# A fused attention-convolution and mixture-of-experts layer on one core: attention in blocks of five rows, all taps spread ahead of the first image, the normalised copy made where it is used

## What is computed

```python
# layer 0, first half: a convolution yields 49 weights per pixel, and these weigh a 7x7 window, dilation 2
u = ln_over_channels(x)
k = relu(conv7x7_dilated2(u, w1) + b1)              # 256 -> 128 channels
k = relu(batchnorm(conv1x1(k, w2) + b2))            # 128 -> 49
attn = softmax(k, axis=1)
out = sum(shift(u, 2*ki, 2*kj) * attn[:, p] for p, (ki, kj) in enumerate(taps))
x = x + out
# second half: tokens are pixels; each of the four batches picks two of eight experts from its mean token
t = tokens(x); tn = ln(t)
rw = softmax(scaled(softmax(mean(tn) @ Wr + br)))   # top 2 of 8, per batch
y = sum_k w_k * (gelu(tn @ W1[k] + b1[k]) @ W2[k] + b2[k])
x = t + ln(y + tn) * gamma + beta
```

## Time and profile before

| | |
|---|---|
| median of three runs | 1289.99 us (1288.7 to 1295.73) |
| profiled execution | 1290.51 us, span 1288.6 us |
| TensorE busy | 1128.8 us (88%) |
| VectorE busy | 715.9 us (56%) |
| ScalarE busy | 496.7 us (39%) |
| GpSimd busy | 237.4 us (18%) |
| mean granted clock of TensorE | 0.898 of 2.4 GHz |
| DMA | 106.34 MB, 83 GB/s on average |

### The profile page before, as it was taken

How to read it: one execution, slowest core, us unless ns; L and a number is a source line. 1 busy time by engine, 2 the same in 40 slices (tenths; PEclk the granted TensorE clock), 3 DMA queues, 4 the chain that set the end, 5 groups by cost and what they waited for, 6 DMA issues and landing times. The chain is left out here.

```text
span 1288.6 us, 19335 instructions
## 1 busy us (share of the span) xinstructions
PE 1128.8 (88%) x7380; PEld 980.9 (76%) x7380; DVE 715.9 (56%) x1719; ACT 496.7 (39%) x923; POOL 237.4 (18%) x160
## 2 busy tenths in 40 slices
PE   3766899999999999939877978689899989989997
PEld 2665667667666666639877968589899989989997
DVE  3445345356355243414673664456777776776776
ACT  4444333232332201114353354364454455455442
POOL 1000000000000000010251353203322331332332
PEclk9969899999999999755885687689999999999999
DMA  9210021112102000060894297404214211421211
GB/s 272 82 37 19 19 74 38 38 39 87 37 1 73 17 1 16 1 134 3 220 264 113 58 269 204 150 25 148 74 50 133 77 51 60 147 73 37 75 50 37
DMA packets 98968, 106.34 MB, mean 83 GB/s; under 512 B 5298, under 2 KB 95699, under 8 KB 98692
## 3 DMA queue, kind: packets, MB, share of 16 engines
q1 hardware_dynamic: 79888, 86.15, 23.4%
q10 hardware_dynamic: 19000, 19.11, 4.8%
HBM read 65.69 MB, written 39.56 MB: 82 GB/s over the span
## 5 line engine op out<-in xcount | busy, mean ns | idle before, releaser
L729 PE MATMUL pM<-V,U 128*128 128x368 f16 (+3 forms) x2016 | 319.3, 315 | 0.0
L729 PEld LDWEIGHTS pM<-V,U 128*128 128x128 f16 x2016 | 196.7, 98 | 107.2 <-issue 0.8
L1507 DVE TENSOR_TENSOR gl<-gf,gh 128x384 fp32r<-128x384 f32 x192 | 161.9, 864 | 63.6 <-ACT gh L1401 63.6
L1401 ACT ACTIVATE gf<-pH,b1c 128x384 f32<-128x384 f32 x192 | 112.0, 583 | 193.3 <-PE pH L1620 143.2
L1635 PE MATMUL pY<-w2h,gh 128*128 128x256 f32 x576 | 167.4, 291 | 17.4 <-DVE z L1519 16.4
L1635 PE MATMUL pY<-w2l,gh 128*128 128x256 f32 x576 | 163.1, 283 | 0.0
L1635 PE MATMUL pY<-w2h,gl 128*128 128x256 f32 x576 | 162.9, 283 | 0.0
L521 DVE TENSOR_TENSOR V<-pV,V 128x384 f16<-128x384 f32 x96 | 53.1, 556 | 179.7 <-ACT V L407 179.4
L1620 PE MATMUL pH<-xh,w1h 128*128 128x384 f32 x384 | 131.5, 343 | 9.3 <-DVE xl L1500 4.6
L407 ACT CAST V<-pV 128x384 f16<-128x384 f32 x96 | 45.6, 477 | 225.8 <-PE pV L700 225.7
L1620 PE MATMUL pH<-xl,w1h 128*128 128x384 f32 x384 | 130.7, 340 | 0.0
(11 more groups left out here) (173 smaller groups left out, 1539.2 us busy)
## 6 DMA issues: line engine op xcount, KB each, us to landing
xa<-in_xt SPq DMA_DIRECT2D x16, 576.0 KB, 5.0
xn_scratch<-xa SPq DMA_DIRECT2D x16, 576.0 KB, 6.0
xn<-xn_scratch SPq DMA_DIRECT2D x16, 576.0 KB, 8.6
xr<-in_xt SPq DMA_DIRECT2D x16, 576.0 KB, 6.3
t_scratch<-ts ACTq DMA_DIRECT2D x16, 576.0 KB, 5.3
tn_scratch<-tn ACTq DMA_DIRECT2D x16, 576.0 KB, 5.3
tnk<-tn_scratch SPq DMA_DIRECT2D x24, 384.0 KB, 3.3
tk<-t_scratch SPq DMA_DIRECT2D x24, 384.0 KB, 3.9
```

The costliest lines, as they stand in the source:

```text
L729: return nc.tensor.matmul(out[:, :, first:end], U[:, hi_u, k, piece, :], V[:, b % 2, hi_v, k, c, :, first + TILES * d:end + TILES * d], st ...
L1401: last = nc.scalar.activation(dst, pH[:, j % 4, 0:CN], ACT.Gelu, bias=b1c[:, j // FB, j % FB:j % FB + 1])
L1507: tt(gl[:, sl, j, :], gf[:, j % 2, :], gh[:, sl, j, :].bitcast(F32), ALU.subtract).then_inc(g_step, 1)
```

## The change

It has four parts.

- **Start-up of the convolution.** Tap turns and image turns alternate: tap turn j of a pair, then image turn j of the next image. The magnitudes, `ln`, `normalise_x` and `tap_scale` get fixed places between them. The batch-norm constants are made after pair 0. `bound` writes to another PSUM bank.
- **Attention blocks.** A block is five rows, 120 tokens (`TB`), and an image has five blocks, the last of four rows. There are 11 pairs (d, h) for 10, `SLOT` is 6 for 4, so a group of eight images has 44 items of six matmuls; `SBANKS` is 3. An image's `attend` has 39 matmuls for 48. Transfers of an image are split in two (four whole blocks and the short one).
- **Spreading first.** `A` has room for both groups. All 88 items are done before image 0; the load of the second group's taps waits for the last item of the first group. The lists in the image loop change: ScalarE `store(n-1)`, `normalise(n-1)`, `x_high(n+2)`; VectorE `sums(n)`, `x_low(n+2)`, `statistics(n)`. `accumulate` covers all images, with two buffers.
- **No `tn` in DRAM.** The attention phase no longer stores it. The expert phase makes `tnk` from `tk`: `statistics` on VectorE, `scale_x` on GpSimd, `normalise` on ScalarE, three chunks ahead. `tk` has three buffers.

The diff, cut to its core:

```diff
@@ conv_phase, VectorE (ScalarE and TensorE have the same form)
-            u_lows(0, 0, U_PAIR)
-            tap_scale(1)
-            v_lows(2)
-            ln(3)
...
+            tap_scale(0)
+            for pair in range(PAIRS_OG):
+                for j in range(U_PAIR):
+                    u_low(U_PAIR * pair + j)
+                    if j < V_TURNS and pair + 1 < BI:
+                        v_low(V_TURNS * (pair + 1) + j)
+                    if j == LN_AT and pair + 2 <= BI:
+                        ln(pair + 2)
+                    if j == SCALE_AT and pair + 1 < PAIRS_OG:
+                        tap_scale(pair + 1)
+                if pair == 0:
...
@@ constants of the attention
+BROWS = 5
+TB = BROWS * SIDE
+NB = -(-SIDE // BROWS)
-SLOT = 4
-SBANKS = OBANKS = 4
+SLOT = 6
+SBANKS, OBANKS = 3, 4
@@ attend_phase, SyncE
-            for n in range(IMGS):
-                if n % GI == 0 and n // GI + 1 < GROUPS:
-                    load_attn(n // GI + 1)
+            load_attn(1)
+            for n in range(2, IMGS):
+                load_xn(n)
+                load_x(n)
@@ attend_phase, ScalarE
-            for n in range(IMGS):
-                if n % GI == 0:
-                    spread_out(act, nc.scalar.copy, n // GI, 0, a_by_act, x_high)
-                    x_high(n + 1)
-                if (n + 1) % GI > 0 and n + 2 < IMGS:
-                    x_high(n + 2)
-                if n > 0:
-                    normalise(n - 1)
-                    store(n - 1)
+            for u in range(0, GROUPS * NU, 2):
+                spread_out(act, nc.scalar.copy, u, a_by_act)
+                if u == NU // 2:
+                    x_high(0)
+            x_high(1)
+            for n in range(IMGS):
+                if n > 0:
+                    store(n - 1)
+                    normalise(n - 1)
+                if n + 2 < IMGS:
+                    x_high(n + 2)
@@ attend_phase, VectorE
             for n in range(IMGS):
...
                 sums(n)
-                if (n + 1) % GI > 0:
-                    statistics(n)
-                    if n + 2 < IMGS:
-                        x_low(n + 2)
+                if n + 2 < IMGS:
+                    x_low(n + 2)
+                statistics(n)
@@ attend_phase, TensorE
+            for item in range(GROUPS * NU):
+                spread_taps(item)
             for n in range(IMGS):
-                if n % GI == 0:
-                    spread_taps(n // GI)
                 attend(n)
@@ ffn_phase, SyncE
-                sp.dma_start(tnk[:, s], tn_d[rows, :].rearrange("(t p) c -> p t c", p=P)).then_inc(tnk_loaded[s], 16)
                 sp.dma_start(tk[:, s], t_d[rows, :].rearrange("(t p) c -> p t c", p=P)).then_inc(tk_loaded[s], 16)
@@ ffn_phase, GpSimd
+                    if later(b, m, 3, CHUNKS):
+                        scale_x(*later(b, m, 3, CHUNKS))
                     rsqrt(b, m)
@@ ffn_phase, ScalarE
+            def normalise(b, m):
+                n, s = CHUNKS * b + m, m % 2
+                act.wait_ge(x_scaled, 2 * (n + 1))
...
+                for t in range(CT):
+                    last = nc.scalar.activation(tnk[:, s, t, :], tk[:, m % TBUFS, t, :], ACT.Identity,
+                                                bias=xsh[:, s, t:t + 1], scale=xrs[:, s, t:t + 1])
+                last.then_inc(tn_made, 2)
+            normalise(0, 0)
+            normalise(0, 1)
             take_x(0, 0)
             split_w1(0)
...
                     if later(b, m, 2, CHUNKS):
                         take_x(*later(b, m, 2, CHUNKS))
+                    if later(b, m, 3, CHUNKS):
+                        normalise(*later(b, m, 3, CHUNKS))
                     if m == CHUNKS - 2 and later(b, m, 2, CHUNKS):
                         split_w1(b + 1)
@@ ffn_phase, VectorE
+            def statistics(b, m):
...
+                for t in range(CT):
+                    s.did(nc.vector.bn_stats(xst[:, t, :], tk[:, m % TBUFS, t, :]))
+                s.settle()
+                carry(nc, spare[0:1, 0:1])
+                for t in range(CT):
+                    s.did(nc.vector.bn_aggr(xmv[:, t, :], xst[:, t, :]))
+                s.settle()
...
+                s.did(nc.vector.tensor_scalar(xve[:, sl], xmv[:, :, 1], 1e-5, None, ALU.add))
+                s.did(nc.vector.tensor_scalar(xnm[:, sl], xmv[:, :, 0], -1.0, None, ALU.mult))
...
                     if later(b, m, 2, CHUNKS):
                         take_x(*later(b, m, 2, CHUNKS))
+                    if later(b, m, 3, CHUNKS):
+                        statistics(*later(b, m, 3, CHUNKS))
                     if m == CHUNKS - 2 and later(b, m, 2, CHUNKS):
                         split_w1(b + 1)
                     sum_up(b, m)
```

More of the change, by code:

```diff
@@ L619, in a_low @@
                        ALU.subtract).then_inc(alo_ready, 1)
-            def v_lows(n):
-                for j in range(V_TURNS):
-                    v_low(V_TURNS * n + j)
-            def u_lows(pair, first, end):
-                for j in range(first, end):
-                    u_low(U_PAIR * pair + j)
             ln(0)
             ln(1)
-            v_lows(0)
-            ln(2)
-            v_lows(1)
-            dve.wait_ge(par_loaded, 16 * 7)
-            s = Steps(dve, bn_step, 0, BN_STEPS)
@@ L648, in _ @@
-            s.settle()
-            s.did(nc.vector.tensor_scalar(w2s[:, :], w2s[:, :], bnp[:, 7:8], None, ALU.mult))
-            s.did(stt(bnp[:, 0:1], bnp[:, 0:1], bnp[:, 7:8], bnp[:, 2:3], ALU.mult, ALU.add))
-            s.at(BN_STEPS)
-            u_lows(2, 0, U_HALF)
-            tap_scale(3)
-            u_lows(2, U_HALF, U_PAIR)
-            v_lows(3)
-            ln(BI)
-            u_lows(3, 0, U_PAIR)
+            for j in range(V_TURNS):
+                v_low(j)
+            tap_scale(0)
@@ new lines, in normalise @@
+                for t in range(NB):
+                    rows = rows_of(t)
+                    last = nc.scalar.activation(tn[0:rows, n % 2, t, :], ts_[0:rows, n % 2, t, :], ACT.Identity,
+                                                bias=shift[0:rows, n % 2, t:t + 1],
+                                                scale=rstd[0:rows, n % 2, t:t + 1])
+                last.then_inc(tn_ready, 1)
+            for u in range(0, GROUPS * NU, 2):
+                spread_out(act, nc.scalar.copy, u, a_by_act)
+                if u == NU // 2:
+                    x_high(0)
@@ L1133, in attend, with spread_taps @@
-            def attend(n):
+            aTv = aT[:, :, :].rearrange("p a (i x) -> p a i x", i=GI)
+            def spread_taps(item):
+                g, u = item // NU, item % NU
+                d, h, k = ITEMS[u]
+                nb = blocks_of(h)
+                if u == 0:
+                    pe.wait_ge(at_loaded, 16 * (g + 1))
+                if item >= SBANKS:
+                    pe.wait_ge(*evicted(item - SBANKS))
+                for w in range(k * SLOT, (k + 1) * SLOT):
+                    at = window(d, h, w) + G0
+                    v = 1 + EDGE.index(w) if w in EDGE else 0
+                    o = (w % SLOT) * 2 * GI * nb
+                    first = h * SIDE + w % MO * TILES + w // MO
+                    last = nc.tensor.matmul(pS[0:TB, item % SBANKS, o:o + 2 * GI * nb], G[:, v, at:at + TB],
+                                            aTv[:, :, :, first:first + (nb - 1) * TB + 1:TB],
+                                            start=True, stop=True)
+                last.then_inc(spread, 1)
@@ L1147, in attend, with sum_tokens @@
                                 start=(k == 0), stop=(k == len(terms) - 1))
                     last.then_inc(o_ready, 1)
-            def sum_tokens(e, c):
-                at = SUM_COLS + c * SUMS + e
-                for t in range(NT):
-                    tokens = acc[:, e, t] if e < B else tn[:, (IMGS - LATE + e - B) % 2, t]
-                    last = nc.tensor.matmul(pS[:, 0, at:at + 1], tokens[:, c * P:(c + 1) * P],
-                                            ones[:, :], start=(t == 0), stop=(t == NT - 1))
-                return last
+            def sum_tokens(b):
+                pe.wait_ge(acc_step, (BI - 1) * (b + 1))
+                for c in range(CC):
+                    at = c * B + b
+                    for t in range(NB):
+                        last = nc.tensor.matmul(pC[:, at:at + 1], acc[:, b % 2, t, c * P:(c + 1) * P], ones[:, :],
+                                                start=(t == 0), stop=(t == NB - 1))
+                last.then_inc(sums_ready, 1)
@@ L1170, in _ @@
-            for e in range(LATE):
-                pe.wait_ge(tn_ready, IMGS - LATE + e + 1)
-                for c in range(CC):
-                    last = sum_tokens(B + e, c)
-            last.then_inc(sums_ready, 1)
+                if n > BI and n % BI == 2:
+                    sum_tokens(n // BI - 1)
+            sum_tokens(B - 1)
 EXPERTS, TOPK, FH = 8, 2, 512
@@ L1411, in _ @@
             split_w2(0)
+            normalise(0, 2)
             def body(b):
```

417 lines of the change are left out of this document (214 added, 203 removed).

## The result

The changed kernel takes 1335.3 us (median of 4 runs, 1330.7 to 1346.4) against 1289.4 for the kernel before: 1.036 times as long, interval 1.029 to 1.043. The forecast was 1325, with 1290 to 1345 as its range. The profiled execution has a span of 1328.9 us against 1288.6, 40.3 longer.

What follows compares the result with a forecast made beforehand. TensorE waits in start-up and attention; in the experts the chain through VectorE decides. From 1290.5: start-up -28, attention +3, expert head +4, chunks +31, batch changes +24 give 1324.5, say 1325 us, range 1290 to 1345.

Steps and rivals of the forecast that it cites:

- Start-up (-28): Convolution start-up: interleaved tap and image turns bring the first product to 116 us instead of 144.2, -28 us.
- Spreading (-9): Attention, spreading the taps: fewer, narrower products plus a gap for the second load, 79.1 us instead of 40.6 + 47.3.
- I therefore let it go by columns, 1.7 ns each: Spread products on TensorE: price proportional to columns, 0.137 us for 80 and 0.111 for 64, 69.9 us in all.
- Rival (c): Spreading: a product costs 0.164 us whatever its width, total 1342 us; chance 0.09.
- Images (+10): Attention's sixteen images: 9.4 us each, 2.9 more for one in four, 143.5 us instead of 133.3.
- the ring itself: Image loop: new order closes a loop of statistics, power, normalisation, `x_high`, `x_low` over one image, 9.4 us.
- Rival (b): Images: the loop does not close, images at 8.3 us or less, -14, total 1311 us; chance 0.11.
- Tail and head (+6): Attention tail 23 us instead of 21 (+2), and expert head later since `tn` is made, not loaded (+4).
- Chunks (+31): Expert chunks: statistics on VectorE between `xl` and `z` add 1.7 us to each of 18 chunks, +31 us.
- nothing covers it: Expert chunks: statistics between `xl` and `z` lie on the chain of waits, so their 1.7 us count fully.
- Changes of batch (+24): Three changes of batch: `split_w1` waits behind `normalise`, TensorE's idle grows from 3.25 to 9 us; 3 x 8, +24.
- Rival (a): Expert stage: statistics are free because VectorE's other waits shorten as much, total 1270 us; chance 0.10.

Runs made afterwards that it cites:

- the run on distances: Changed kernel with 96 stationary columns in spread products and moving columns read at many strides: 0.080 us a product at 8 bytes, 0.137 at 192, 0.160 at 240.
- the statistics alone: Kernel before plus only the eight statistics instructions per chunk on VectorE between `xl` and `z`, results unread: 1337.6 us, 1.040 of before.
- the kernel with the statistics between the `gl`: Changed kernel with each chunk's statistics in five pieces behind `gl` of the chunk before, its load issued one chunk earlier: 1294.1 us, 1.005 of before.
- the run open on VectorE alone: Changed kernel with only VectorE's image order put back, `statistics(n)` before `x_low(n+2)`; ScalarE still normalises before `x_high`: 1311.0 us, one run.

## Why the forecast was right, and where not

**Start-up (-28).** Right; 116 us was forecast for the first product, 112.1 came in the profile and 114.5 to 116.8 in the ten other kernels with this start-up.

**Spreading (-9).** Wrong in sign: +2.7. The step that failed is "I therefore let it go by columns, 1.7 ns each". I had seen that the price hung on the distance of the columns, and then left it as it was while the change moved that distance from 192 to 240 bytes; in the run on distances, the same form of product costs 0.137 us at 192 and 0.160 at 240. 80 columns took 0.160 us and not 0.137 (432 x 0.023 = 9.9 us), 64 took 0.117 and not 0.111 (0.6), and the gap was 9.8 and not 8.3 us (1.5): together 12 of the 12 us missed. Rival (c), 0.164 whatever the width, was near in price but wrong in its reason, as the 64 columns show.

**Images (+10).** Right to 2 us, as to period (9.2 to 9.3 for 9.4), to the accumulation (+2.9) and to the ring itself. Rival (b) was mis-sized: -14 for an open ring, where it gives -31.5.

**Tail and head (+6).** Mis-sized: +2.5. Which of its terms was too large was not followed up.

**Chunks (+31).** The mechanism and its 1.7 us are right (19.58 us in the first batch; the statistics alone reproduce it). The term was mis-sized since it had no clock in it: 42.4. It also counted 18 chunks where the stretch holds 17 (the first statistics stand ahead of the first `z`), so 29 us are the instructions and some 13 the clock. TensorE waits 1.7 to 3.9 us for `z` in every chunk that is not a change of batch, and with that come stretches at 1.2 GHz, nearly all of them in the batches behind a change; 33.2 us of work ran there instead of 6.5. The "nothing covers it" holds for the place between `xl` and `z` alone.

**Changes of batch (+24).** The gap was forecast at 9 us and is 8.7 to 9.1. The whole term is 18.5: part of what I charged here for the clock falls into the chunk behind, and stands in the line above.

The sum was 6 us short: 12 too little for the spreading, 11 for the chunks (13 of clock, less the chunk counted too much) and 2 for the images, and 19 too much in the other four lines of the table. The forecast was near the time partly because these errors had both signs. Rival (a), free statistics, was wrong for where they were put and nearly right for the gaps between the `gl`.

## What to carry to other kernels

Before an instruction is put into a queue, follow the chain of waits once around: on the chain 1.7 us of VectorE cost 1.7 us in each of 21 chunks and TensorE's clock besides, and in gaps further up, between the `gl`, the same work cost 0.1 to 0.2. When two engines each take a step of image n+2 in front of a step of image n, look for the ring this closes; one engine's order put back is enough to open it. And what is moved in front of a queue's other work counts with its DMA issues: a pair of stores cost 1.0 us an image by the timeline for the wait and the issue alone.

## What was not expected of the hardware

- The distance of moving columns sets the pitch of small products: for 80 fp16 columns 0.080 us at 8 bytes or less (with 96 stationary ones), 0.144 at 16, 0.137 at 64, 128 and 192, 0.143 at 232, 0.163 at 208, 0.160 at 240, all at 1.2 GHz.
- A VectorE instruction on 128x3 elements, 0.17 us elsewhere, took 1.80 us at 877.29 in the kernel with the statistics between the `gl`, in the stretch in which GpSimd runs its two additions; one `gl` there took 1.42 for 0.56. In the kernel before, 47 of the 192 `gl` took over 0.8 us, and all 47 overlap one of these additions.
- In the profile of the kernel after, TensorE's clock held at 2.4 GHz through the first batch with waits of 1.7 us in every chunk, and fell in some chunks of the later batches, with waits of 2.0 to 3.9. In the run open on VectorE alone, with the same expert code, it fell in the first batch too, behind a wait of 1.73 us (0.50 from 851.6 to 854.8). What decides it was not tried.
